# Graph network kernel, second message pass: VectorE computes a group's messages first and adds the preceding group's sums last

## What is computed

```python
h = silu(emb @ mlp_w0 + mlp_b0)
h = silu(h @ mlp_w1 + mlp_b1)
w = (h @ mlp_w2 + mlp_b2).reshape(-1, 4, MUL)
ss = xs[senders]
vv = xv[senders]
m0 = w[:, 0] * ss
m1 = w[:, 1][:, :, None] * ss[:, :, None] * Y1[:, None, :]
m2 = w[:, 2][:, :, None] * vv
m3 = w[:, 3] * (einsum('emc,ec->em', vv, Y1) / SQ3)
msg_s = segment_sum(concatenate([m0, m3], axis=1), receivers)
msg_v = segment_sum(concatenate([m1, m2], axis=1), receivers)
```

## Time and profile before

| | |
|---|---|
| time of three runs, us | 2977.77, 2978.21, 2989.45; median 2978.21 |
| profiled execution, us | span 2979.6, its own time; 1.4 above that median |
| TensorE busy | 1851.9 us, 62% |
| VectorE busy | 1673.9 us, 56% |
| GpSimd busy | 1569.1 us, 53% |
| ScalarE busy | 1271.8 us, 43% |
| second pass | from the first gather of L490, 1621.84 us, to the last addition, 2957 us |

### The profile page before, as it was taken

One profiled execution on the slowest core, in us unless ns is written; L12 is line 12 of the kernel. 1 busy time (PEld: TensorE's weight loads), 2 busy tenths in 40 slices (PEclk: granted clock), 3 DMA queues, 4 the chain that ended last, 5 costly groups with the idle time before them and its releaser, 6 DMA issues. The chain is left out here.

```text
span 2979.6 us, 37370 instructions
## 1 busy us (share of the span) xinstructions
PE 1851.9 (62%) x9706; PEld 1441.9 (48%) x9706; DVE 1673.9 (56%) x4970; ACT 1271.8 (43%) x3058; POOL 1569.1 (53%) x1617
## 2 busy tenths in 40 slices
PE   3255454454554554454568177778787887887787
PEld 2244344354443444444555055555555555555556
DVE  2355555555554555554666055666656655666668
ACT  0245444455454555454545033434334334334345
POOL 4345455555555555555302756666666666666640
PEclk7556666656666666666678577888888778888889
DMA  6456454545555555544301211111111111111110
GB/s 213 135 140 170 134 136 133 138 135 144 142 137 137 140 143 138 145 130 134 109 2 35 53 39 43 45 47 44 45 45 44 45 44 44 44 44 46 46 36 24
DMA packets 242944, 271.84 MB, mean 91 GB/s; under 512 B 46236, under 2 KB 201970, under 8 KB 242220
## 3 DMA queue, kind: packets, MB, share of 16 engines
q0 software_dynamic: 64480, 158.57, 19.7%
q1 hardware_dynamic: 178252, 110.87, 13.6%
HBM read 257.11 MB, written 12.15 MB: 90 GB/s over the span
## 5 line engine op out<-in xcount | busy, mean ns | idle before, releaser
L476 POOL DMA_INDIRECT rows<-kv_tab,src_col x806 | 766.9, 951 | 691.5 <-DVE msg L1048 438.6
L490 POOL DMA_INDIRECT rows<-up_tab,src_col x806 | 796.4, 988 | 488.4 <-DVE rows L1362 240.9
L706 PE MATMUL ps<-hotT,rows 128*128 128x128 f32 x3232 | 511.1, 324 | 314.5 <-DVE rows L1369 164.5
L706 PEld LDWEIGHTS ps<-hotT,rows 128*128 128x128 f32 x3232 | 486.6, 235 | 365.4 <-DVE rows L1369 191.0
L524 PE MATMUL ps<-qwin,hotT 128*128 128x128 f32 x1616 | 357.4, 384 | 404.9 <-issue 194.5
L1333 DVE TENSOR_TENSOR acc<-acc,ps 128x256 f32 x808 | 338.1, 418 | 352.3 <-remote 207.1
L524 PEld LDWEIGHTS ps<-qwin,hotT 128*128 128x128 f32 x1616 | 320.1, 289 | 432.0 <-issue 335.7
L1065 DVE TENSOR_TENSOR acc<-acc,ps 128x128 f32 x808 | 228.0, 282 | 421.8 <-remote 329.4
L533 PE MATMUL ps<-hots,msg 128*128 128x128 f32 x1616 | 334.2, 373 | 48.9 <-DVE msg L1048 28.8
L533 PEld LDWEIGHTS ps<-hots,msg 128*128 128x128 f32 x1616 | 294.5, 273 | 81.3 <-DVE msg L1048 49.3
L757 ACT ACTIVATE hotT<-rel,consts 128x512 f32<-128x512 bf16 x202 | 145.0, 718 | 418.0 <-DMA qwin<-q_tab 303.6
(11 more groups left out here) (169 smaller groups left out, 2192.2 us busy)
## 6 DMA issues: line engine op xcount, KB each, us to landing
qwin<-q_tab SPq DMA_DIRECT2D x808, 64.0 KB
rel<-rel_far SPq DMA_DIRECT2D x202, 128.0 KB
rows<-kv_tab,src_col POOLq DMA_INDIRECT x806
rows<-up_tab,src_col POOLq DMA_INDIRECT x806
rows<-emb_rows SPq DMA_DIRECT2D x202, 16.0 KB
weights<-r_far SPq DMA_DIRECT2D x25, 128.0 KB
emb_rows<-weights SPq DMA_DIRECT2D x25, 128.0 KB
kv_tab<-rows SPq DMA_DIRECT2D x12, 256.0 KB, 2.8
```

Source lines behind the costliest of these rows:

```text
L476: nc.gpsimd.indirect_dma_start(kvr[:, q % RING, k, :], None, kv_tab, bass.IndirectOffsetOnAxis(src_col[:, t:t + 1].bitcast(U32), 0)).then_ ...
L490: nc.gpsimd.indirect_dma_start(upr[:, q % RING, k, :], None, up_tab, bass.IndirectOffsetOnAxis(src_col[:, t:t + 1].bitcast(U32), 0)).then_ ...
L706: mm = pe.matmul(ps[:, 4 + 2 * (q % 2) + k // 2, (2 * (k % 2) + m) * P:(2 * (k % 2) + m + 1) * P], left[:, q % 2, k, :], hot2[:, q % 2, k, ...
```

## The change

In VectorE's slot the messages of group q come first, all eight operations, and the four additions of group q-1 come last in a row. Among the eight, the order changes a little too: the product that raises `g_used` stands ahead of the second sum over directions, and the wide product into `MA` ahead of the last narrow one into `MB`. The semaphore `w_used` is gone; TensorE waits for `msgs_ready` of group q-2 in its place, which the last product raises.

```diff
             def edge_weights(q):
                 pe.wait_ge(h2_sb, q // 2 + 1)
                 if q >= 2:
-                    pe.wait_ge(w_used, q - 1)
+                    pe.wait_ge(msgs_ready, q - 1)
...
                 v.tensor_tensor(tb[:, 2 * b], vyb[:, :, 0], vyb[:, :, 1], ALU.add).then_inc(t1_ready, 1)
-                if q:
-                    add2(q - 1, 0, base)
                 if q >= 2:
                     dve.wait_ge(sum2_ready, QT * (q - 1))
                 v.tensor_tensor(MA[:, b, :, 0:32], w[:, :, 0:32], ss, ALU.mult)
+                v.tensor_tensor(MB[:, b, :, 32:128].rearrange("p t (c m) -> p t c m", c=3),
+                                w[:, :, 64:96].unsqueeze(2).to_broadcast([P, QT, 3, 32]), vv, ALU.mult).then_inc(g_used, 1)
                 dve.wait_ge(t1_ready, q + 1)
                 v.tensor_tensor(tb[:, 2 * b + 1], tb[:, 2 * b], vyb[:, :, 2], ALU.add).then_inc(t2_ready, 1)
-                if q:
-                    add2(q - 1, 1, base)
-                v.tensor_tensor(MB[:, b, :, 32:128].rearrange("p t (c m) -> p t c m", c=3),
-                                w[:, :, 64:96].unsqueeze(2).to_broadcast([P, QT, 3, 32]), vv, ALU.mult).then_inc(g_used, 1)
-                if q:
-                    add2(q - 1, 2, base)
-                dve.wait_ge(t2_ready, q + 1)
-                v.tensor_tensor(MB[:, b, :, 0:32], w[:, :, 96:128], tb[:, 2 * b + 1], ALU.mult).then_inc(w_used, 1)
                 dve.wait_ge(u_ready, q + 1)
                 v.tensor_tensor(MA[:, b, :, 32:128].rearrange("p t (c m) -> p t c m", c=3),
-                                ub[:, b].unsqueeze(2).to_broadcast([P, QT, 3, 32]), y, ALU.mult).then_inc(msgs_ready, 1)
+                                ub[:, b].unsqueeze(2).to_broadcast([P, QT, 3, 32]), y, ALU.mult)
+                dve.wait_ge(t2_ready, q + 1)
+                v.tensor_tensor(MB[:, b, :, 0:32], w[:, :, 96:128], tb[:, 2 * b + 1], ALU.mult).then_inc(msgs_ready, 1)
                 if q:
-                    add2(q - 1, 3, base)
+                    for k in range(QT):
+                        add2(q - 1, k, base)
```

More of the change, by code:

```diff
@@ L304, in build @@
         h1_mm, h1_sb, h2_mm, h2_sb, w_mm = sem("h1_mm"), sem("h1_sb"), sem("h2_mm"), sem("h2_sb"), sem("w_mm")
-        hot2_ready, u_ready, vy_ready, t1_ready, t2_ready, w_used, msgs_ready, g_used = (
-            sem("hot2_ready"), sem("u_ready"), sem("vy_ready"), sem("t1_ready"), sem("t2_ready"), sem("w_used"), sem("msgs_ready"), sem("g_used"))
+        hot2_ready, u_ready, vy_ready, t1_ready, t2_ready, msgs_ready, g_used = (
+            sem("hot2_ready"), sem("u_ready"), sem("vy_ready"), sem("t1_ready"), sem("t2_ready"), sem("msgs_ready"), sem("g_used"))
         sum2_ready, acc2_step, acc2_zero = sem("sum2_ready"), sem("acc2_step"), sem("acc2_zero")
```

## The result

The changed kernel takes 2966.45 us (median of four runs, 2964.86 to 2968.79) against 2981.58 for the kernel before on the same chip (four runs, 2977.77 to 2989.45): ratio 0.9945, 95% interval [0.9927, 0.9963]. It is faster, by 15 us or half a per cent, where 58 were forecast. The number is inside the range, and is the 2966 that rival 3 (half of the gain given back) worked out; the size of the main term was wrong.

What follows compares the result with a forecast made beforehand. The second pass was taken as bound by the gathers plus GpSimd's stops on a full ring, caused by late TensorE completions. 2979.6 - 66 (earlier slot release) + 7 (additions in a row) gave 2920 us, range 2840 to 2985.

Steps and rivals of the forecast that it cites:

- rival 3: Whole kernel: no change, about 2973 us; 2966 if half of the 66 us is given back and the slot costs 12 + 7; chance 0.18.
- What bounds the kernel: Second pass: TensorE's completions arrive late while GpSimd gathers without pause, so the ring fills and GpSimd stops, 240.9 us in 76 waits.
- L1362 comes earlier, -66 us: Second pass, VectorE: the product freeing a ring slot comes 0.87 us sooner at each of 76 stops, -66 us.
- low bound: Bound on the gain from the earlier slot-freeing product: 0, if a later stop gives every microsecond back.
- Messages without the sums of q-1, counted 0: Second pass: messages need only sums of q-2, so TensorE can go one group further; nothing counted beyond the stops.
- TensorE's wait for the last product: Sign in the second pass's profile after: TensorE's waits for the last product fall well below 161.6 us.
- the head: Start of the second pass, where 64 gathers need no free slot: stays starved, 0, bounds -10 and +10 us.
- Additions in a row: VectorE's slot grows from 3.74 to 4.45 us; covered by gathers except in 16 groups behind the last gather, +7 us.
- TensorE's wait for the bank: TensorE, before reusing an edge-weight bank: now waits for all products of q-2, which sums ahead already awaited; 0.
- Rival 1: Second pass: a third of the 76 stops go altogether, 58 us more gained, 2862 us; chance 0.27.
- Rival 2: Second pass: waits still sum to 241 us and VectorE's longer slot costs 12 + 7 us, 2999 us; chance 0.15.

Runs made afterwards that it cites:

- E16: Changed kernel, second pass: one GpSimd memset a group to group 49, two to 99, then none, two gathers of four from 150; 2853.78 us, kernel before 2987.72.
- E5: The kernel before, nothing edited, run again in a sitting where it took 2245.26 us (the short condition): 2239.41 us, one run.
- E6: The changed kernel, nothing edited, run again in the short condition: 2245.52 us against 2245.26 for the kernel before, ratio 0.9999.
- E8: Changed kernel with two of each group's four second-pass gathers left out: 2148.20 us, against 2054.55 for the kernel before with the same cut.
- E9: Changed kernel, additions alternating with the next group's vector product and direction sums, two of four second-pass gathers left out: 2050.96 us, kernel before 2237.57.
- E12: Changed kernel with three of each group's four second-pass gathers: 2645.56 us, against 2715.28 for the kernel before with the same cut.
- E15: Kernel before, second pass: one GpSimd memset a group to group 49, two to 99, then none, two gathers of four from 150; 2847.36 us, unedited 2987.72.
- E13: Kernel before, GpSimd memsets by group: none to 49, one of 256 columns to 99, one of 512 to 149, then two of 512; 2326.27 us, unedited 2242.81.

## Why the prediction was wrong, point by point

- **What bounds the kernel.** Right for the condition that it was read in: late reports, full ring, stop. In E16 they went with a memset between the gathers and came back without it. That they go with uninterrupted gathers alone was too strong: in the short condition (E5) GpSimd gathers without a rest for 1000 us and nothing is late.
- **L1362 comes earlier, -66 us.** The failed step is "over 76 stops", 0.87 each. The 0.87 held for the stops behind 12 gathers, which alone gained: 3.95 to 3.12 us in the mean, 0.83. The 33 short stops were not the same event with other numbers. Their rhythm had cost less per group before (6.1 us against 6.46), and nearly all settled at 6.2. Measured: 28 us by the gaps, 32 by the wait's row, where 66 were forecast. What the prediction gave as its low bound, that a later stop gives the time back, happened to the short stops. Why the runs of gathers grew to 12 was not tested.
- **Not foreseen: the gathers themselves.** 806 of them take 804.8 us and not 796.4, 8 us of the missing gain. That is one trace of each kernel; whether the change or chance made them longer is not shown (in the short condition E5 has 764.9 us and E6 770.3).
- **Messages without the sums of q-1, counted 0.** Right for the time. The sign that was named, TensorE's wait for the last product well below 161.6 us, came true in part by luck: 53.8 of the 82 us are one wait of the head. In the middle 29 us went, and 73.6 us of new waits for ScalarE's L899 took their place.
- **Additions in a row.** Right: the slot measured 4.54 where 4.45 was said, and E8 and E9 show the whole price, 93.65 us or 202 x 0.46, if nothing covers it. Behind the last gather it cost the 7 us of the forecast; what that stretch took fell by 3.3 us for other reasons, so it grew by 3.8. By the page "VectorE: DVE Perf Modes" of the Trainium skill, section "The DRAIN you can't avoid", a semaphore between chained operations costs nothing extra (measured there on eight copies). E8's rows do not bear that out for these additions: each second pair waits 0.20 us for the one before, and in E9 the same additions with other work between them cost nothing. Whether the semaphore or the register step ahead of each addition makes the wait is not told apart.
- **TensorE's wait for the bank, the head:** 0 and +1.1 us, as said. The final stage grew by 1.6 us, which was not counted.
- **Rival 1** (many stops go altogether): 75 became 62, by runs that grew longer, and nothing came of it. The argument against it, that the stop is only put off, was right.
- **Rival 2** (slower at full pace) had the right mechanism, its price too low (0.33 us a group, 0.46 in E8) and its condition wrong: it decides where nothing else is slower than 4.5 us, as in E8, and nowhere in the full kernel.
- **Rival 3** described what happened, for the wrong reason in part: not 12 us lost at full pace but 8 in the gathers. That its 2966 is the measured time is chance.

The sum by what was measured: start +1.1, gathers +8.4, small gaps +0.6, stops -28.0, behind the last gather +3.8, final +1.6, together -12.5; the spans differ by 12.6.

## What to carry to other kernels

When a stall is one beat of a rhythm, work out a cycle, run plus stop over the groups it moves, and not the saving times the number of stops: a shorter stop may go with another rhythm, as here. An order with a longer slot can even win (E12, by 70 us); that it does so by spacing the gathers is a reading. And before an order is tuned against a wait, look whether the wait is there in another sitting; here the whole object of the change was missing in five of eight.

## What the hardware showed that was not expected

- One program, one chip, two times: 2985.02 us in one sitting on chip 2 and 2242.81 in the next, a third more, while single operations of VectorE and single gathers keep their length within 5% (TensorE's follow its clock). Each sitting stayed in its condition. The cause was not found.
- In the long condition TensorE's completions reach VectorE so late that it stands for up to 22 us while GpSimd issues indirect DMAs back to back. A memset of 0.54 us after every second one brings them back in time in the changed order (E16), and only partly in the order before (E15), one run each.
- A memset of half the columns (256) costs a group 0.41 us in E13, that of 512 columns 0.45, so halving it saves little.
